# A state-space stage: tanh in place of SiLU, the norm's sums on ScalarE, another split of the state between TensorE and VectorE

## The chip, the cores and the metric

The kernel runs on one core of one Trainium2 chip. The metric is the device time of one execution in microseconds: 6,593.0 us, median of three runs (6,588.21 to 6,606.39), for the kernel before.

## The reference

The program is a decoder of two layers on an input of 128 sequences of 64 tokens with 128 features: a state-space block, an MLP, attentions, two mixtures of experts. The change touches the first block alone. What that block computes, in short:

```python
def state_space_block(x):                       # per sequence: [T=64, D=128]
    h = rmsnorm(x, input_norm_w)                # x * rsqrt(mean(x*x) + 1e-5)
    xi, z = split(h @ in_proj_W)                # 256 and 256 channels (E = 256)
    xi = silu(causal_conv4(xi) + conv_b)
    dt = clip(softplus(xi @ dt_W + dt_b), 1e-3, 0.1)
    Bt, Ct = xi @ B_W, xi @ C_W                 # N = 64 states per channel
    A = -exp(A_log)
    for t in range(T):                          # state: [E, N]
        state = exp(dt[t] * A) * state + dt[t] * xi[t] * Bt[t]
        y[t] = state @ Ct[t]
    return x + (y * silu(z)) @ out_proj_W
```

## The kernel before

The function `mamba` is the first stage of `build`; all other stages follow behind a barrier and are untouched. It goes through 16 chunks of 8 sequences. A chunk has 64 time steps `t`, of which 63 update the state (1 to 63). The state of a chunk is a [128, 1024] array in PSUM: 128 partitions are two times 64 states, 1024 columns are 4 pairs of sequences by 256 channels. Two such arrays take turns (banks UB to UB+3, by `t % 2`), a bank holds 512 columns.

In a step the engines do this:

- **TensorE**: `add_decayed(i, t)` (L1171) adds, with a product by the unit matrix, the decayed old state into columns 768 to 1023 (`PE_PART`) of the new one; `contract(i, t-1)` (L1175, products at L1183) forms the output by the C matrix; `products` (L1141) makes the step sizes for the exponential of step t+3 (decay product, L1151, bank pair DT) and the input term of step t+1 (input product, L1166). Then a side product, if the step has one. Products of 128 columns of weights go by quarters of 32 (`by_quarters`, L1134), four at a time.
- **ScalarE**: `decay` (L1380), the exponential of 1024 columns of PSUM into `dA`, a ring of four; then small copies out of the one bank PJ that side products write (`take_...`), casts, and at t = 3 the SiLU of 2048 columns (`silus`, L1407).
- **VectorE**: `decay_pe_part` (L1722, TensorE's columns: dA times old state), `add_part` (L1738, twice: its own product added to the new state of step t-1), `decay_part` (L1729, twice). Its own columns are 0 to 511 and 512 to 767 (`DVE_PARTS`). Once in 16 steps it adds the residual (`output`, L1745) and forms one small sum (`weigh_bc`, L1713), once in a chunk, at t = 24, the norm's mean square of chunk i+2 (`norm`, L1697 to L1707).
- **GpSimd**: the rest of the norm (`norm_scale`, `scale`), `step_size` (11 instructions on 1024 columns, softplus as a polynomial), the splitting of operands into three bf16 pieces (`own_rows`, `split_rest`, `split_lo`), the gate by silu(z) (`gate`).
- **SyncE**: loads, stores, and `spread_pieces`, 21 DMAs that lay the pieces out as weights.

The order is written out by hand: every engine's program is the same loop over `t`, with side work hung at fixed `tl = t % 16` of fixed quarters `j = t // 16`, and semaphores tie them. Each engine works through its queue in order. Side products for chunk i+1 and i+2 are in TensorE's queue at: turn_u at tl 1 (every quarter), project_bc at 2, turn_y at 4, project_out at 6; the step-size projections of i+1 at t = 7 to 10 and the C projection at 12, 13; the turn of i+2 at t = 40, its first conv at 42 to 45, its second at 55 to 58, the gates' product at 59, 60, 62, 63. Each group of them writes bank PJ, and the next one waits until ScalarE (or VectorE) took the one before. The waits that matter: `decay_pe_part(t)` waits for `add_decayed(t-1)`; `add_decayed(t)` for `decay_pe_part(t)`; the input product of step t+1 for all of VectorE's products of step t, as it overwrites the state that they read; the decay product of t+3 for the exponential of t+2, with one pair of banks for all.

Chunk 0 and the last three stand outside a loop, 12 chunks inside one of three iterations of four. In the last two chunks the side work for chunks that don't exist is missing.

Of the kernel before, what the change touches and what calls it, by code (L numbers as in the profile page):

```python
# [18 lines left out]
ALU = mybir.AluOpType  # L19
# [880 lines left out]
def mamba(nc, sems, ps, dram, x_in, x_out):  # L900
# [9 lines left out]
    with ExitStack() as mem:  # L910
# [42 lines left out]
        stats = st.sb("stats", [128, 4, 6])  # L953
        mv = st.sb("mv", [128, 4, 2])
# [3 lines left out]
        eps = st.sb("eps", [128, 4])  # L958
        seen = st.sb("seen", [128, 1])
# [11 lines left out]
        set_pool = st.counter("set_pool", 6)  # L971
        passed = st.counter("passed")
        sp_passed = st.counter("sp_passed")
        set_act = st.counter("set_act", 2)
# [9 lines left out]
        xz_ready = st.counter("xz_ready")  # L984
# [66 lines left out]
        with nc.Block() as block:  # L1051
# [78 lines left out]
            def _(pe):  # L1130
# [10 lines left out]
                def products(dt, ub):  # L1141
# [12 lines left out]
                    if ub:  # L1154
                        i, t = ub
                        s, tl = t // 16 % 2, t % 16
                        if t >= 2:
                            pe.wait_ge(md_ready.sem, md_ready.at(i, 2 * (t - 1)))
                        else:
                            pe.wait_ge(md_ready.sem, md_ready.at(i - 1, 2 * (T - 1 - t)))  # L1160
                        if tl == 0:
                            pieces_here(i, t // 16)
                        for pl in range(2):
                            for g in range(2):
                                k = slice(64 * g, 64 * g + 64)
                                mm = nc.tensor.matmul(ps[:, UB + 2 * (t % 2) + g, 256 * pl:256 * pl + 256],  # L1166
# [4 lines left out]
                def add_decayed(i, t):  # L1171
                    pe.wait_ge(mp_ready.sem, mp_ready.at(i, t))
                    by_quarters(state(t, PE_PART), ident, m[:, t % RING, PE_PART], False, True, False).then_inc(hp_ready.sem, 1)

# [82 lines left out]
                def first():  # L1257
# [26 lines left out]
                    products((0, 1), None)  # L1284
                    products((0, 2), (0, 0))

                def chunk(i, u, lead, lead2, trail):
                    for t in range(T):
                        j, tl = t // 16, t % 16
                        k = 4 * i + j  # L1290
                        if 1 <= t < T - 1:
                            add_decayed(i, t)
# [73 lines left out]

                def last():
# [8 lines left out]
            def _(act):  # L1376
# [5 lines left out]

                def take_turn(i):
# [8 lines left out]
                def take_conv(i, f):  # L1392
# [4 lines left out]
                                         bias=conv_b[:, f:f + 1]).then_inc(in_taken.sem, 1)  # L1397

                def take_gates(i, half):
                    act.wait_ge(in_done.sem, in_done.at(i, half + 3))  # L1400
                    nc.scalar.copy(raw[:, 1024 + 512 * half:1536 + 512 * half], ps[:, PJ, :]).then_inc(in_taken.sem, 1)
# [66 lines left out]
                def first():  # L1468
                    act.wait_ge(w_loaded.sem, w_loaded.at(0))
                    nc.scalar.copy(sel[:], sel_f[:]).then_inc(set_act.sem, 1)  # L1470
                    nc.scalar.activation(a_neg[:], a_neg[:], ACT.Exp).then_inc(set_act.sem, 1)
                    act.wait_ge(set_pool.sem, set_pool.at(0))
                    act.wait_ge(set_dve.sem, set_dve.at(0))
                    for i in range(2):
                        take_turn(i)
                        for f in range(2):
                            take_conv(i, f)
                        for half in range(2):
                            take_gates(i, half)
                        if i == 0:  # L1480
                            silus(0, 0)
# [12 lines left out]
                def chunk(i, u, lead, lead2, trail):  # L1494
                    for t in range(T):
# [5 lines left out]
                        behind = j > 0 or trail  # L1501
                        if j == 0 and tl == 0 and lead and trail:
# [6 lines left out]
                        if j == 0 and tl == 3 and lead:  # L1509
                            silus(i + 1, 1 - u)  # L1510
# [45 lines left out]
            def _(pool):  # L1556
                def norm_scale(i):
                    pool.wait_ge(normed.sem, normed.at(i))
                    nc.gpsimd.tensor_tensor(nrstd[:], msq[:], eps[:], ALU.add).then_inc(nrstd_ready.sem, 1)
# [3 lines left out]
                def scale(i):  # L1563
# [5 lines left out]
                    ins.then_inc(scaled.sem, 1)  # L1569

# [64 lines left out]
                def first():  # L1635
                    nc.gpsimd.memset(half_neg[:], -0.5).then_inc(set_pool.sem, 1)
                    nc.gpsimd.memset(eps[:], NORM_EPS).then_inc(set_pool.sem, 1)
# [6 lines left out]
                    for i in range(2):  # L1644
                        norm_scale(i)
                        scale(i)
                    for n in range(1, LP_STEPS + 1):
# [7 lines left out]
                def chunk(i, u, lead, lead2, trail):  # L1655
                    for t in range(T):
# [6 lines left out]
                        if j < 2 or lead:  # L1663
# [7 lines left out]
                            elif tl == 12:  # L1671
                                direct(ip, jp)
                        if lead and j == 0 and tl >= 11:
# [6 lines left out]
                        if lead2 and j == 1:  # L1680
                            if tl == 13:
                                norm_scale(i + 2)
                            elif tl == 14:
# [8 lines left out]
            def _(dve):  # L1692
                def norm(i):
                    dve.wait_ge(x_loaded.sem, x_loaded.at(i))
                    dve.wait_ge(nrstd_ready.sem, nrstd_ready.at(i - 1, 1))
                    for j in range(4):
                        ins = nc.vector.bn_stats(stats[:, j], x[:, j])  # L1697
                    ins.then_inc(normed.sem, 1)
                    dve.wait_ge(normed.sem, normed.at(i, 1))
                    nc.vector.tensor_copy(seen[:], stats[:, 0, 0:1])  # L1700
                    for j in range(4):
# [2311 lines left out]
```

## Time and profile before

| | |
|---|---|
| median of three runs | 6,593.0 us |
| profiled execution | 6,625.31 us |
| its span, first to last instruction | 6,623.4 us |
| VectorE busy over the span | 5,054.2 us (76%) |
| TensorE busy over the span | 5,086.3 us (77%) |
| ScalarE busy over the span | 3,374.8 us (51%) |
| GpSimd busy over the span | 3,163.8 us (48%) |
| exponentials (L1380), 1,008 of them | 1,125.2 us busy, 1,116 ns each |

In the rows DVE is VectorE, PE is TensorE (its weight loads are PEld), ACT is ScalarE, POOL is GpSimd. Instructions overlap at their ends, so the distance from start to start says what one costs in a row of them; the duration is longer.

### The profile page before, as it was taken

How to read it: one execution, taken by the hardware profiler on the slowest of the kernel's cores; microseconds unless marked ns; L12 is line 12 of the kernel's file. 1: busy time of each engine (PE TensorE's matmuls, PEld its weight loads, DVE VectorE, ACT ScalarE, POOL GpSimd, SP SyncE). 2: the span in 40 equal slices, each digit the busy share in tenths (PEclk: the TensorE clock that was granted, in tenths of full speed). 3: DMA queues.
4: the chain of work that ended last, by engine and by line, in shares of the span. 5: the costliest groups of instructions: out<-in, count | busy, mean ns of one | idle time of the engine just before them, and what ended most of it. 6: DMA issues, size and time to landing. Idle time of an engine off the chain costs nothing. (4 is left out here: it accounts for less than half of the span.)

```text
span 6623.4 us, 173241 instructions
## 1 busy us (share of the span) xinstructions
PE 5086.3 (77%) x60580; PEld 2997.0 (45%) x60580; DVE 5054.2 (76%) x10431; ACT 3374.8 (51%) x4743; POOL 3163.8 (48%) x2904
## 2 busy tenths in 40 slices
PE   4888888888888886686876965999956648777890
PEld 1333333333333334465664633666745536666440
DVE  3999999999999995697965345777769938888334
ACT  3666666666666654355751211444446617777440
POOL 5433333334443313465643564555523318889443
PEclk8999999999999998798988987999978859999995
DMA  1111111111111112221121632000011112222343
GB/s 42 41 45 47 43 46 41 49 41 40 48 41 46 42 39 82 59 58 36 44 72 55 149 106 60 18 17 18 13 29 34 28 43 73 73 73 74 121 136 102
DMA packets 620483, 368.00 MB, mean 56 GB/s; under 512 B 67337, under 2 KB 601292, under 8 KB 619852
## 3 DMA queue, kind: packets, MB, share of 16 engines
q1 hardware_dynamic: 600524, 335.54, 18.2%
q0 software_dynamic: 11648, 21.26, 1.6%
q8 instruction: 352, 5.77, 0.4%
q10 hardware_dynamic: 7680, 3.15, 0.2%
q14 instruction: 279, 2.29, 0.1%
HBM read 204.83 MB, written 66.85 MB: 41 GB/s over the span
## 5 line engine op out<-in xcount | busy, mean ns | idle before, releaser
L1380 ACT ACTIVATE mb_dA<-ps,mb_a_neg 128x1024 f32<-128x1024 f32 x1008 | 1125.2, 1116 | 905.7 <-PE ps L1151 690.0
L1729 DVE TENSOR_TENSOR mb_m<-mb_dA,ps 128x512 f32<-128x512 f32 x2016 | 1034.2, 562 | 0.0
L1738 DVE TENSOR_TENSOR ps<-mb_m,ps 128x512 f32<-128x512 f32 x1984 | 1025.8, 570 | 0.0
L1134 PE MATMUL ps<-mb_m,mb_ident 128*32 128x256 f32 x7936 | 645.7, 398 | 55.7 <-DVE mb_m L1722 55.0
L1183 PE MATMUL ps<-mb_m,mb_cz 128*32 128x256 f32 x8064 | 640.5, 390 | 16.9 <-DVE mb_m L1729 6.5
L1166 PE MATMUL ps<-mb_ur,mb_bl 64*128 64x256 bf16 x4032 | 401.8, 278 | 187.0 <-DVE mb_m L1729 175.4
L1722 DVE TENSOR_TENSOR mb_m<-mb_dA,ps 128x256 f32<-128x256 f32 x1008 | 432.5, 429 | 96.9 <-PE ps L1134 54.7
L1151 PE MATMUL ps<-mb_ur,mb_sel 64*128 64x256 bf16 x4032 | 405.1, 280 | 80.8 <-ACT mb_dA L1380 59.9
L1183 PEld LDWEIGHTS ps<-mb_m,mb_cz 128*32 128x32 f32 x8064 | 261.9, 113 | 220.7 <-issue 54.1
L1151 PEld LDWEIGHTS ps<-mb_ur,mb_sel 64*128 64x128 bf16 x4032 | 115.8, 95 | 522.7 <-issue 282.3
L1134 PEld LDWEIGHTS ps<-mb_m,mb_ident 128*32 128x32 f32 x7936 | 192.6, 110 | 320.4 <-issue 171.2
L677 POOL TENSOR_TENSOR x_p<-x_p,x_rec 128x2048 f32<-128x2048 f32 x64 | 231.8, 3622 | 211.7 <-DVE x_rec L838 211.5
L1166 PEld LDWEIGHTS ps<-mb_ur,mb_bl 64*128 64x128 bf16 x4032 | 147.1, 96 | 377.5 <-DVE mb_m L1729 364.2
L1631 POOL TENSOR_TENSOR mb_ys<-mb_ys,mb_cbu 128x256 f32<-128x256 f32 x64 | 47.0, 734 | 539.5 <-ACT mb_ys L1461 539.5
L1618 POOL TENSOR_TENSOR mb_rest<-mb_tm,mb_pc 128x768 f32<-128x768 f32 x64 | 105.8, 1653 | 366.9 <-ACT mb_pc L1439 366.9
L677 POOL TENSOR_TENSOR ea_p<-ea_p,ea_rec 128x2048 f32<-128x2048 f32 x70 | 253.6, 3622 | 37.6 <-DVE ea_rec L838 36.8
L3174 POOL TENSOR_TENSOR gq_qr<-gq_qc,gq_qs 128x1024 f32<-128x1024 f32 x64 | 151.0, 2359 | 240.1 <-DVE gq_qs L3221 222.5
L2505 POOL DMA_INDIRECT mx_tk<-moe_normed,moe_tokens x156 | 147.9, 948 | 187.6 <-POOLq L68 103.4
L487 PE MATMUL ps<-x_ident,x_p 128*128 128x128 f32 x1024 | 162.4, 310 | 61.8 <-POOL x_p L677 61.8
L599 ACT ACTIVATE x_p<-x_p 128x2048 f32<-128x2048 f32 x64 | 122.0, 1907 | 163.1 <-DVE x_p L828 163.0
L2577 DVE TENSOR_TENSOR mx_gu<-mx_gate,ps 128x512 f32<-128x512 f32 x78 | 53.5, 686 | 191.5 <-ACT mx_gate L2562 146.9
L606 ACT COPY x_pT<-ps 128x1024 f32<-128x1024 f32 x128 | 129.3, 1010 | 137.1 <-PE ps L487 136.1
(497 smaller groups left out, 13202.6 us busy)
## 6 DMA issues: line engine op xcount, KB each, us to landing
mb_ur<-mb_pc SPq DMA_DIRECT2D x768, 64.0 KB
mb_bl<-mb_pc SPq DMA_DIRECT2D x576, 64.0 KB
ef_w<-in_ef_w SPq DMA_DIRECT2D x35, 514.5 KB
mx_w<-in_mx_w SPq DMA_DIRECT2D x39, 384.0 KB
moe_made<-mx_y SPq DMA_DIRECT2D x39, 256.0 KB
ea_wqk<-in_ea_wqk SPq DMA_DIRECT2D x70, 129.0 KB
ea_wvo<-in_ea_wvo SPq DMA_DIRECT2D x70, 128.5 KB
ea_x<-hidden SPq DMA_DIRECT2D x280, 32.0 KB, 2.0
```

Source lines behind the costliest of these rows:

```text
L487: mm = nc.tensor.transpose(ps[:, 6 + c0 // 512, c0 % 512:c0 % 512 + 128], P_g[:, u, g, t, 2 * jj:2 * jj + 2, :].rearrange("p h k -> p (h k ...
L677: nc.gpsimd.tensor_tensor(v, v, rec[:].rearrange("p (c a) -> p c a", a=1).to_broadcast([128, 32, 64]), ALU.mult).then_inc(p_ready.sem, 1)
L1134: mm = nc.tensor.matmul(out[c:c + 32], weights[:, c:c + 32], moving, start=start, stop=stop, skip_group_check=not grouped)
L1151: mm = nc.tensor.matmul(ps[:, DT + g, 256 * pl:256 * pl + 256], sel[k, pl], ur[k, t // 16 % 2, t % 16], start=True, stop=True)
L1166: mm = nc.tensor.matmul(ps[:, UB + 2 * (t % 2) + g, 256 * pl:256 * pl + 256], bl[k, s, tl, 128 * pl:128 * pl + 128], ur[k, s, tl], start=g ...
L1183: mm = nc.tensor.matmul(ps[32 * pr:32 * pr + 32, YB, 0:E], cz[:, j % 2, pr, 32 * tl:32 * tl + 32], m[:, t % RING, 256 * pr:256 * pr + 256] ...
L1380: nc.scalar.activation(dA[:, t % RING].rearrange("p (g n) -> p g n", g=2), ps[:, DT:DT + 2, :], ACT.Exp, scale=a_neg[:, 0:1]).then_inc(dA_ ...
L1722: nc.vector.tensor_tensor(m[:, t % RING, PE_PART], dA[:, t % RING, PE_PART], state(t - 1, PE_PART), ALU.mult).then_inc(mp_ready.sem, 1)
L1729: nc.vector.tensor_tensor(m[:, t % RING, cols], dA[:, t % RING, cols], state(t - 1, cols), ALU.mult).then_inc(md_ready.sem, 1)
L1738: nc.vector.tensor_tensor(h, m[:, t % RING, cols], h, ALU.add).then_inc(hd_ready.sem, 1)
L2505: nc.gpsimd.indirect_dma_start(tk[:, i % DEEP, t], None, xn_rows, bass.IndirectOffsetOnAxis(ap=tokens[:, 4 * i + t:4 * i + t + 1], axis=0) ...
L3174: nc.gpsimd.tensor_tensor(qr[:, t], qc[:, t], qs[:, t], ALU.add).then_inc(q_turned.sem, 1)
```

## The change

- SiLU is made as h·tanh(h) + h with h = half the argument: ScalarE's copies into `raw` halve (`scale=0.5`, and `conv_b` is halved in the set-up), ScalarE makes tanh in four pieces of 512 columns (`tanh_half`, at t = 2, 3, 6, 7), and GpSimd multiplies and adds (`gated`, at t = 2, 4, 7, 9). `project_dt` waits piece by piece.
- The norm's sum of squares is made by ScalarE (`norm`: four Squares with a sum, at t = 26 to 29) in place of VectorE's statistics; GpSimd's `norm_scale` and `scale` come one step later.
- The parity of the state's banks is (t + u) % 2 with u the parity of the chunk, so the first state of a chunk no longer lies where the last but one of the chunk before does; the input products of a chunk's steps 0 and 1 are issued in steps 62 and 63 of the chunk before.
- TensorE's `products` (decay and input product) come behind the step's side product, not ahead of it.
- `PE_PART` is 384 columns (640 to 1023), `DVE_PARTS` are 0 to 319 and 320 to 639; the second lies over the border of two banks.

```diff
-        PE_PART = slice(768, 1024)
-        DVE_PARTS = [slice(0, 512), slice(512, 768)]
-
-        def state(t, cols):
-            g = cols.start // 512
-            return ps[:, UB + 2 * (t % 2) + g, cols.start - 512 * g:cols.stop - 512 * g]
+        PE_PART = slice(640, 1024)
+        DVE_PARTS = [slice(0, 320), slice(320, 640)]
+
+        def state(u, t, cols):
+            bank = UB + 2 * ((t + u) % 2)
+            return ps[:, bank:bank + 2, :].rearrange("p g n -> p (g n)")[:, cols]
...
                         else:
-                            pe.wait_ge(md_ready.sem, md_ready.at(i - 1, 2 * (T - 1 - t)))
+                            pe.wait_ge(md_ready.sem, md_ready.at(i - 1, 2 * (T - 2 + t)))
...
                 def project_dt(i, u, e, f):
+                    if e == 0:
+                        pe.wait_ge(xz_ready.sem, xz_ready.at(i, f + 1))
                     if f == 0:
-                        if e == 0:
-                            pe.wait_ge(xz_ready.sem, xz_ready.at(i))
-                        else:
+                        if e == 1:
                             pe.wait_ge(dtp_taken.sem, dtp_taken.at(i, 1))
...
-                        dt = (i, t + 3) if t + 3 < T else (i + 1, t + 3 - T) if lead and t + 3 > T else None
-                        ub = (i, t + 1) if t + 1 < T - 1 else (i + 1, 0) if lead and t == T - 1 else None
-                        products(dt, ub)
 
                         ahead = j < 2 or lead
                         behind = j > 0 or trail
...
                             elif tl in (11, 12, 14, 15):
                                 gates(i + 2, {11: 0, 12: 1, 14: 2, 15: 3}[tl])
 
+                        dt = (i, t + 3) if t + 3 < T else (i + 1, t + 3 - T) if lead and t + 3 > T else None
+                        if t < T - 2:
+                            products(dt, (i, t + 1) if t else None, u)
+                        else:
+                            products(dt, (i + 1, t + 2 - T) if lead else None, 1 - u)
+
...
+                def norm(i, j):
+                    act.wait_ge(x_loaded.sem, x_loaded.at(i))
+                    act.wait_ge(nrstd_ready.sem, nrstd_ready.at(i - 1, 1))
+                    act.wait_ge(xT_done.sem, xT_done.at(i - 1))
+                    nc.scalar.activation(xn[:, j], x[:, j], ACT.Square, accum_out=msq[:, j:j + 1]).then_inc(
+                        normed.sem, 1)
...
-                def silus(i, u):
-                    act.wait_ge(in_taken.sem, in_taken.at(i))
+                def tanh_half(i, u, q):
+                    act.wait_ge(in_taken.sem, in_taken.at(i, q + 1))
                     act.wait_ge(bc_done.sem, bc_done.at(4 * (i - 2) + 3))
                     act.wait_ge(yz_ready.sem, yz_ready.at(4 * (i - 2) + 3))
-                    nc.scalar.activation(xz[:, u], raw[:], ACT.Silu).then_inc(xz_ready.sem, 1)
+                    nc.scalar.activation(xz[:, u, 512 * q:512 * q + 512], raw[:, 512 * q:512 * q + 512],
+                                         ACT.Tanh).then_inc(tanh_ready.sem, 1)
...
+                def gated(i, u, q):
+                    pool.wait_ge(tanh_ready.sem, tanh_ready.at(i, q + 1))
+                    part, half = xz[:, u, 512 * q:512 * q + 512], raw[:, 512 * q:512 * q + 512]
+                    nc.gpsimd.tensor_tensor(part, part, half, ALU.mult).then_inc(xz_scaled.sem, 1)
+                    pool.wait_ge(xz_scaled.sem, xz_scaled.at(i, q + 1))
+                    nc.gpsimd.tensor_tensor(part, part, half, ALU.add).then_inc(xz_ready.sem, 1)
```

In the set-up, ahead of the first step, ScalarE's four Squares of chunk 0 wait for GpSimd's clearing of tiles, and GpSimd makes the four pieces of chunk 0 between the norm of chunk 0 and that of chunk 1.

## Rows read from the trace of the kernel before

**Rows 1.** The page: busy time by engine, and TensorE's granted clock in 40 slices.

```profile
PE 5086.3 (77%) x60580; PEld 2997.0 (45%) x60580; DVE 5054.2 (76%) x10431; ACT 3374.8 (51%) x4743; POOL 3163.8 (48%) x2904
...
PEclk8999999999999998798988987999978859999995
```

**Rows 2.** Groups by line and shape, whole span; last, the summary of line L1722.

```profile
L1722 DVE TENSOR_TENSOR mb_m<-mb_dA,ps 128x256 f32<-128x256 f32 x1008 | 432.5, 429 | 96.9 <-PE ps L1134 54.7 <-PE ps L1166 27.1 <-issue 5.9
...
L828 DVE TENSOR_TENSOR ea_p<-ps,ea_top 128x2048 f32<-128x2048 f32 x70 | 160.4, 2291 | 2.4
...
L1580 POOL TENSOR_TENSOR mb_lp<-mb_lp,mb_ex 128x1024 f32<-128x1024 f32 x64 | 151.4, 2366 | 2.8
...
L3630 ACT ACTIVATE ef_hid<-ps,ef_w 128x512 f32<-128x512 f32 x140 | 96.4, 689 | 25.8 <-PE ps L3588 24.5
...
L1425 ACT COPY mb_tm<-ps 128x512 f32<-128x512 f32 x64 | 37.5, 587 | 13.8 <-PE ps L1235 13.2
...
L1722 DVE TENSOR_TENSOR mb_m<-mb_dA,ps x1008: 410/422/517, 113.9 to 2496.3; 128x256 f32<-128x256 f32 x168
```

**Rows 3.** VectorE's timeline at the norm: start, duration (us), line, tiles, shape.

```profile
1069.64 0.42 DVE L1722 TENSOR_TENSOR mb_m<-mb_dA,ps 128x256 f32<-128x256 f32 x1
1069.97 1.02 DVE L1738 TENSOR_TENSOR ps<-mb_m,ps 128x512 f32<-128x512 f32 x2
...
1071.83 0.87 DVE L1697 BATCH_NORM_STATS2 mb_stats<-mb_x 128x6 f32<-128x128 f32 x4
...
1075.73 0.42 DVE L1722 TENSOR_TENSOR mb_m<-mb_dA,ps 128x256 f32<-128x256 f32 x1
```

**Rows 4.** Timeline of all engines over one step with a conv product.

```profile
1002.94 0.39 PE L1151 MATMUL ps<-mb_ur,mb_sel 64*128 64x256 bf16 x4
...
1003.17 0.38 PE L1166 MATMUL ps<-mb_ur,mb_bl 64*128 64x256 bf16 x4
1003.46 1.12 ACT L1380 ACTIVATE mb_dA<-ps,mb_a_neg 128x1024 f32<-128x1024 f32 x1 [0.77 <-PE ps L1151]
...
1003.48 1.07 PE L1134 MATMUL ps<-mb_xT,mb_w_conv 128*32 128x512 f32 x8
...
1004.37 0.61 PE L1134 MATMUL ps<-mb_m,mb_ident 128*32 128x256 f32 x8
...
1004.62 0.69 ACT L1395 ACTIVATE mb_raw<-ps,mb_conv_b 128x512 f32<-128x512 f32 x1
1004.80 0.61 PE L1183 MATMUL ps<-mb_m,mb_cz 128*32 128x256 f32 x8
...
1005.05 0.42 DVE L1722 TENSOR_TENSOR mb_m<-mb_dA,ps 128x256 f32<-128x256 f32 x1
1005.34 0.11 PEld L1151 LDWEIGHTS ps<-mb_ur,mb_sel 64*128 64x128 bf16 x4 [0.41 <-issue]
```

**Rows 5.** TensorE's timeline: the turn of the step-size operand and what follows.

```profile
1131.82 0.66 PE L1235 MATMUL ps<-mb_ident,mb_du 128*128 128x128 f32 x4
1132.41 0.64 PE L1134 MATMUL ps<-mb_m,mb_ident 128*32 128x256 f32 x8
```

**Rows 6.** ScalarE's timeline at the SiLU of one chunk.

```profile
1022.72 1.28 ACT L1407 ACT_TABLE_LOAD   x1
1024.01 1.91 ACT L1407 ACTIVATE mb_xz<-mb_raw 128x2048 f32<-128x2048 f32 x1
1025.94 1.28 ACT L1380 ACT_TABLE_LOAD   x1
```

**Rows 7.** VectorE's timeline over the same SiLU: the first product of three steps.

```profile
1025.37 0.42 DVE L1722 TENSOR_TENSOR mb_m<-mb_dA,ps 128x256 f32<-128x256 f32 x1
...
1029.75 0.42 DVE L1722 TENSOR_TENSOR mb_m<-mb_dA,ps 128x256 f32<-128x256 f32 x1 [2.11 <-PE ps L1134]
...
1033.74 0.41 DVE L1722 TENSOR_TENSOR mb_m<-mb_dA,ps 128x256 f32<-128x256 f32 x1
```

**Rows 8.** GpSimd's timeline in the set-up: the first step_size instruction.

```profile
56.25 2.77 POOL L1586 TENSOR_SCALAR mb_ex<-mb_ex 128x1024 f32<-128x1024 f32 x1 [18.32 <-ACT mb_ex L1417]
```

More of the change, by code:

```diff
@@ L1139, in pieces_here, with products @@
                     pe.wait_ge(pieces_loaded.of(j % 2), pieces_loaded.at(4 * i + j, j % 2))
-                def products(dt, ub):
+                def products(dt, ub, v):
                     if dt:
@@ L1283, in first @@
                     project_bc(0, 0, 1)
-                    products((0, 1), None)
-                    products((0, 2), (0, 0))
+                    products((0, 1), (0, 0), 0)
+                    products((0, 2), (0, 1), 0)
                 def chunk(i, u, lead, lead2, trail):
@@ L1471, in first @@
                     nc.scalar.activation(a_neg[:], a_neg[:], ACT.Exp).then_inc(set_act.sem, 1)
+                    nc.scalar.activation(conv_b[:], conv_b[:], ACT.Identity, scale=0.5).then_inc(set_act.sem, 1)
                     act.wait_ge(set_pool.sem, set_pool.at(0))
                     act.wait_ge(set_dve.sem, set_dve.at(0))
+                    act.wait_ge(set_act.sem, set_act.at(0))
+                    for j in range(4):
+                        norm(0, j)
                     for i in range(2):
                         take_turn(i)
+                        if i == 0:
+                            for j in range(4):
+                                norm(1, j)
                         for f in range(2):
@@ L1480, in first @@
                         if i == 0:
-                            silus(0, 0)
+                            for q in range(4):
+                                tanh_half(0, 0, q)
                             for e in range(2):
@@ L1501, in chunk @@
                         behind = j > 0 or trail
+                        if j == 1 and tl in (10, 11, 12, 13) and lead2:
+                            norm(i + 2, tl - 10)
                         if j == 0 and tl == 0 and lead and trail:
@@ L1646, in first @@
                         scale(i)
+                        if i == 0:
+                            for q in range(4):
+                                gated(0, 0, q)
                     for n in range(1, LP_STEPS + 1):
@@ L1672, in chunk @@
                                 direct(ip, jp)
+                        if lead and j == 0 and tl in (2, 4, 7, 9):
+                            gated(i + 1, 1 - u, {2: 0, 4: 1, 7: 2, 9: 3}[tl])
                         if lead and j == 0 and tl >= 11:
@@ L1692, in _ @@
             def _(dve):
[L1693 to L1701, printed above, removed]
-                        ins = nc.vector.bn_aggr(mv[:, j], stats[:, j])
-                    ins.then_inc(normed.sem, 1)
-                    dve.wait_ge(normed.sem, normed.at(i, 2))
-                    nc.vector.tensor_tensor(msq[:], mv[:, :, 0], mv[:, :, 0], ALU.mult).then_inc(normed.sem, 1)
-                    dve.wait_ge(normed.sem, normed.at(i, 3))
-                    nc.vector.tensor_tensor(msq[:], msq[:], mv[:, :, 1], ALU.add).then_inc(normed.sem, 1)
                 def weigh_bc(i, j):
@@ L1736, in add_part @@
                     cols = DVE_PARTS[g]
-                    h = state(t, cols)
+                    h = state(u, t, cols)
                     nc.vector.tensor_tensor(h, m[:, t % RING, cols], h, ALU.add).then_inc(hd_ready.sem, 1)
@@ L1772, in chunk @@
                         if t >= 1:
-                            decay_part(i, t, 0)
-                            decay_part(i, t, 1)
-                        if lead2 and j == 1 and tl == 8:
-                            norm(i + 2)
+                            decay_part(i, u, t, 0)
+                            decay_part(i, u, t, 1)
                         if tl == 11:
```

56 lines of the change are left out of this document (27 added, 29 removed).

## The prediction

> **What bounds the kernel now.** The page comes first: no engine is busy over 77% of the span [rows 1], so shares decide nothing, and the change touches one stage, the state-space scan (its first step starts at 113.9 us, its last at 2,496.3: 16 chunks of 63 steps, 1,008 in all [rows 2]). In VectorE's timeline of that stage a plain step is five instructions back to back: the TensorE part's product, 0.33 us later two sums and then two other products, 1.86 later the next instruction, 2.19 us in all and no idle [rows 3]. VectorE is the pace, and what makes a step longer is visible as a gap ahead of its first product (L1722). Over all steps these gaps sum to 96.9 us [rows 2]. A chunk takes 150 us (first to last start is 2,382 us, and the last chunks are shorter), of which 63 steps of 2.19 are 138. The other 12, by the starts of L1722 in every chunk: 3.9 at the norm on VectorE, 4.2 at the SiLU, 1.3 at the border, 2.6 in steps with side products or with small instructions of VectorE's own.
>
> **The change, part by part** (against the profiled execution, 6,625.3 us, 0.5% above the median of 6,593.0; the sum is then taken from the median).
>
> *Columns.* VectorE handles 256+768+768 = 1,792 columns a step before, 384+640+640 = 1,664 after. The starts [rows 3] give 0.33 for one instruction of 256 and 0.93 (half of 1.86) for two of together 768, so 1.05 ns a column and 0.06 an instruction: 128 columns are 0.13 us, and a step becomes 2.06. In 992 steps (a chunk's first has no sums): **-129 us**. The new slices of 320 lie over a border of PSUM banks. No row of the scan shows VectorE doing that; its instruction on 2,048 columns of PSUM passes three such borders and takes 2,291 ns, what 1.05 ns a column and a fixed part give [rows 2]. I take no penalty; the other end is 0.05 an instruction (the fixed part once more), two a step: +100.
>
> *Norm.* The 14 norms inside the scan stand between two steps of VectorE: 1,069.64 to 1,075.73 is 6.09, 3.90 over a step [rows 3]. They go: **-55**. ScalarE gets four Squares of 128 columns in four steps. No row shows one; a copy of 512 columns takes 0.59 [rows 2], an upper end, against 0.94 free beside the exponential of 1.12 in a step of 2.06. Nothing then waits for them (POOL's part is moved one step, and the turn that needs it is 20 steps on). Range 0 to +5.
> The Trainium skill (ScalarE: Activation LUTs, Rules for kernel authors) speaks against this move: multiplies belong on VectorE, which is up to three times faster. By rows a Square costs no more than 0.59 on an engine with room, and the sum has 0 for it; by the page's preference the norm would stay and the 55 us with it.
>
> *SiLU.* One activation of 2,048 columns stands with a table load before and one after between two exponentials [rows 6]; VectorE needs 8.37 for two steps (1,025.37 to 1,033.74) instead of 4.38 [rows 7], 4.2 on the mean of 15. The gap ended at TensorE's add, which waited for the exponential. These go: **-63**. In their place ScalarE makes four tanh pieces, about 0.6 each by the copy of 512. In the fullest step, 7, one stands behind a cast of 768 columns: 1.4 against 0.94 free, made good in the next two. GpSimd multiplies and adds 512 columns four times: 2.37 us for 1,024 [rows 2], so 2.4 a piece and 9.6 a chunk. GpSimd's queue is then: piece, own_rows, piece, split_rest, piece, split_lo, piece, and it is free near step 12, as the first step_size can start. The projections at steps 7 and 8 need pieces 0 and 1, ready about steps 5 and 7. Hidden; the other end is +1 a chunk, +15.
> The Trainium skill (the same page, What ACT_TABLE_LOAD costs) gives a switch 2.66 us with its drain. The load here takes 1.28 and the activation starts 0.01 behind it [rows 6], so the trace disagrees; by the page the stall would be some 2.7 larger and this term about -105.
>
> *TensorE.* Its step, in a row of start times [rows 4]: decay product to input product 0.23, to the side product 0.31, side product (conv, 512 columns) 0.89, unit product 0.43, contraction to the next decay product 0.54: 2.40, so 1.51 without a side product. The unit product has four passes on 256 columns in 0.43; 384 columns add 0.21. After: 1.72 a plain step, 2.61 with 512 columns, 2.31 with a turn (0.59 [rows 5]) and 2.18 with a short projection (about half of the conv's, 0.46). Against 2.06 TensorE loses 0.55, 0.25 and 0.12 and gains back 0.34. It may fall behind before VectorE feels it: unit product 0.60 after the step's start (the product's 0.42, 0.13 for its new columns, 0.05 for the semaphore), 0.68+0.21 = 0.88 to the next product (0.68: 1,004.37 to 1,005.05 [rows 4]), so 2.06-1.48 = 0.58.
> The new order puts the side product ahead of the decay product, and thus of ScalarE's exponential. Where one side product needs the bank that ScalarE clears of the one before (steps 1 to 2 of every 16, 8 to 9, and 10 to 11 in the last 16), the way is: decay product to exponential 0.52, exponential 1.12, take 0.59 to 0.69, 2.3 to 2.4 with the semaphores; TensorE is back there after 0.23+0.31+0.64+0.54 = 1.72. It waits 0.6 to 0.7.
> Going through a chunk with these: 0.38 at each step 2 (four times); the dt and c group (steps 7 to 13) 0.09+0.55+1.24+0.55+0.21+0.55; the first conv group 0.52+0.55+0.55; the second with the gates 0.09+3x0.55+0.78+0.09. That is 9.5 with the steps at 2; VectorE's own small instructions in the same steps hide 1.3, so 8.2; before, the same groups cost 1.4. So 6.9 in each of 14 chunks, 4 in the 15th, about nothing in the last: **+101**. Ends: +54 if the waits for ScalarE don't come (3.7 a chunk), +160 if nothing of TensorE's lag is hidden (11.3).
>
> *Border.* With the parity kept over it, the next chunk's first input product no longer waits for the last product. L1722's idle behind L1166 is 27.1 us over the run [rows 2], about 0.6 at each of 12 plain borders and more at the first steps; it goes, but the second step still waits for unit product, contraction and exponential in a row. **-7**, between -20 and +5.
>
> *Set-up.* GpSimd stood idle 18.32 us until step_size [rows 8]. Now four pieces (9.6) and the second norm (about 3.5) stand before it, which began 4 us ahead of that point, and ScalarE's first Squares wait for GpSimd's clearing. **+6**, between 0 and +10.
>
> Sum: -129-55-63+101-7+6 = -147. From 6,593: **6,446 us**, 2.2% faster.
>
> **Rivals.**
> *TensorE keeps up*: the waits for ScalarE fall into slack; +54 instead of +101: 6,399. For it: most single side products now leave no mark at 2.19. Against: conv steps are at 2.40 now [rows 4], and they get longer.
> *Nothing is hidden*: +160 instead of +101: 6,505. For it: the lag allowed is only 0.58. Against: two of four conv steps are absorbed now.
> *The table loads stay*: tanh not in the exponential's table. Each piece would bring two loads, 1.12+2.57+0.6 in a step of 2.06, some 9.3 a chunk where 4.2 is now: +77 instead of -63 is +140, 6,586, no change. Against: the Relu of a later stage runs behind exponentials with idle time that TensorE alone ends, no load [rows 2].
> The Trainium skill (ScalarE: Activation LUTs, Table sets) lists tanh and relu in the set of exp, which gives this rival its small chance; no run here shows tanh.
> *ScalarE and TensorE in a ring, slower than before*: every side product, not six of 35 in a chunk, waits for ScalarE, because the exponential now starts behind the side product and each take behind the exponential. 29 more waits of 0.7 in 15 chunks are +300: 6,750. It decides from 147/(29x15) = 0.34 us for each. Against: most side products have a step without one behind them, and TensorE's way to the second next is 3.4, over the 2.4 needed.
>
> **How the numbers follow.** Forecast 0.56, TensorE keeps up 0.19, nothing hidden 0.14, table loads stay 0.04, ring 0.05, else 0.02 (a penalty at the bank border is in the last and in the third). The range takes the first three with their bounds, 6,385 to 6,510; the small ends of norm, SiLU and border lie in it. A measurement of this kernel tells 0.3% (20 us) from no change: faster 0.90, within 0.05, slower 0.05.
>
> **What would show it.** L1722's starts 2.06 apart in plain steps; products of 320 columns near 0.49 each, or longer if the bank border costs; no load of a table between 122 and 2,230 us; no gap at steps 6 and 24; periods of 2.6 in conv steps; TensorE idle behind ScalarE's copy at steps 2 and 9. TensorE's granted clock, nine tenths with some eights in the stage's slices [rows 1], should be no lower, as long idle stretches at steps 6 and 24 are gone. The prediction is wrong if plain steps are not at 2.06, or if side steps cost far from 7 us a chunk more.

## The result: 1.4% faster, with more of the gain eaten than forecast

The changed kernel takes 6,504.2 us (median), the kernel before 6,591.9 measured beside it: ratio 0.9857, 95% interval 0.9838 to 0.9876, so 82 to 107 us less. The forecast was 6,446, in a range of 6,385 to 6,510. Two executions of one later run (ScalarE's copies first) took more than twice the usual time, 14,057 and 14,334 us, and are left out. The profiled execution has a span of 6,481.9 us. Its page of the profile:

```profile
PE 5194.2 (80%) x60580; PEld 2995.8 (46%) x60580; DVE 4876.1 (75%) x10255; ACT 3334.8 (51%) x4888; POOL 3324.5 (51%) x3031
...
PEclk8999999999999998898979977999978859999995
```

VectorE has lost 178 us of work against [rows 1], TensorE has gained 108, GpSimd 161; the granted clock in the stage's slices is as before. The groups by line that answer to [rows 2] (the first two parts of VectorE's work and its sums):

```profile
L1739 DVE TENSOR_TENSOR mb_m<-mb_dA,ps 128x384 f32<-128x384 f32 x1008 | 552.8, 548 | 191.4 <-PE ps L1132 140.3 <-ACT mb_dA L1381 40.7 <-issue 9.0
L1746 DVE TENSOR_TENSOR mb_m<-mb_dA,ps 128x320 f32<-128x320 f32 x2016 | 883.7, 479 | 0.0
L1755 DVE TENSOR_TENSOR ps<-mb_m,ps 128x320 f32<-128x320 f32 x1984 | 879.1, 488 | 0.0
...
L1739 DVE TENSOR_TENSOR mb_m<-mb_dA,ps x1008: 537/547/556, 117.6 to 2400.3; 128x384 f32<-128x384 f32 x168
```

Where VectorE waited 96.9 us ahead of its first product [rows 2], it now waits 191.4, nearly all for TensorE's unit product (L1132) and for the exponential (L1381). The scan starts 3.7 us later (117.6 against 113.9) and its last step starts 96.0 earlier (2,400.3 against 2,496.3). The medians are 88 apart, so the scan has the whole of the change. The spans of the two profiled executions are 141.5 apart, and should not be compared: 45.5 of that lies behind the scan, in stages that the change does not touch. These stages take 4,082 us in this one execution, 4,127 in the kernel before and 4,120 to 4,132 in all runs below; why they were shorter here stays open.

The starts of VectorE's first product in each of the 63 steps, in medians over the 12 chunks of the loop, add up to this (us per chunk; the length of step t is the distance to the start of the next one; the forecast's column is put together here from the terms of its steps, 2.06 for a plain one, with VectorE's own small instructions as measured):

| steps | before | after | forecast |
|---|---|---|---|
| border: 63, 1, 2, 3 | 9.37 | 10.52 | 8.7 |
| 4 to 8 (the SiLU's) | 15.68 | 10.49 | 10.5 |
| 9 to 15 (dt and c projections) | 15.87 | 17.50 | 17.5 |
| second and third of the other quarters: 18, 19, 34, 35, 50, 51 | 13.13 | 15.13 | 13.5 |
| 43 to 47 (first conv) | 11.46 | 11.99 | 11.9 |
| 57 to 62 (second conv, gates) | 13.62 | 14.89 | 14.9 |
| the other 30 (with the norm's step) | 70.57 | 62.42 | 62.5 |
| all | 149.70 | 142.95 | 139.5 |

Two lines, the border and the quarters, hold the whole miss of 3.4 us a chunk: 1.8 and 1.6. One quarter's start in full, in the timeline of all engines (start, duration, idle before and what ended it):

```profile
1021.59 0.54 DVE L1739 TENSOR_TENSOR mb_m<-mb_dA,ps 128x384 f32<-128x384 f32 x1
...
1021.86 1.12 ACT L1381 ACTIVATE mb_dA<-ps,mb_a_neg 128x1024 f32<-128x1024 f32 x1 [0.71 <-PE ps L1149]
...
1022.19 0.85 PE L1132 MATMUL ps<-mb_m,mb_ident 128*32 128x384 f32 x8
...
1022.88 0.36 ACT L1471 COPY mb_ys<-ps 128x256 f32<-128x256 f32 x1
...
1023.34 0.64 PE L1181 MATMUL ps<-mb_m,mb_cz 128*32 128x256 f32 x8 [0.30 <-issue]
1023.64 0.55 DVE L1739 TENSOR_TENSOR mb_m<-mb_dA,ps 128x384 f32<-128x384 f32 x1
1023.91 0.66 PE L1233 MATMUL ps<-mb_ident,mb_du 128*128 128x128 f32 x4
...
1025.96 0.55 DVE L1739 TENSOR_TENSOR mb_m<-mb_dA,ps 128x384 f32<-128x384 f32 x1 [0.18 <-PE ps L1132]
1026.02 0.58 ACT L1435 COPY mb_tm<-ps 128x512 f32<-128x512 f32 x1
...
1026.65 0.64 PE L1132 MATMUL ps<-mb_w_bc,mb_xz 128*32 128x128 f32 x16 [0.33 <-ACT mb_tm L1435]
...
1028.69 0.56 DVE L1739 TENSOR_TENSOR mb_m<-mb_dA,ps 128x384 f32<-128x384 f32 x1 [0.59 <-PE ps L1132]
```

TensorE waits twice for ScalarE. The unit product starts at 1,022.19; the contraction behind it could start 0.66 later, at 1,022.85, but it opens a new sum in the one bank for outputs and waits until ScalarE has copied the old one out. That copy (L1471) stands behind the exponential and ends at 1,023.24; the contraction starts at 1,023.34. (The view puts the last 0.30 of this gap down to "issue"; the kernel has the wait, and the run with ScalarE's copies first, below, takes it away.) Then the projection at 1,026.65 waits for the copy (L1435) of the turn ahead of it. The second wait was in the forecast, the first was not, and both fall in a stretch where TensorE has no lag to spare: 2.31 and 2.73 us for two steps of 2.06.

The border, same view:

```profile
1126.03 0.55 DVE L1739 TENSOR_TENSOR mb_m<-mb_dA,ps 128x384 f32<-128x384 f32 x1
...
1126.38 1.12 ACT L1381 ACTIVATE mb_dA<-ps,mb_a_neg 128x1024 f32<-128x1024 f32 x1 [0.57 <-PE ps L1149]
...
1127.55 0.39 PE L1149 MATMUL ps<-mb_ur,mb_sel 64*128 64x256 bf16 x4 [0.41 <-ACT mb_dA L1381]
1127.87 0.85 PE L1132 MATMUL ps<-mb_m,mb_ident 128*32 128x384 f32 x8
...
1128.79 0.55 DVE L1739 TENSOR_TENSOR mb_m<-mb_dA,ps 128x384 f32<-128x384 f32 x1 [1.41 <-PE ps L1132]
1129.08 0.59 ACT L1409 ACTIVATE mb_raw<-ps 128x512 f32<-128x512 f32 x1
...
1129.71 0.66 PE L1233 MATMUL ps<-mb_ident,mb_du 128*128 128x128 f32 x4 [0.99 <-ACT mb_raw L1409]
```

Step 1 starts with no gap, as the new parity should have it. But the decay product of step 3 stands ahead of the unit product of step 1 in TensorE's queue, and it waits for the exponential of step 2: the gap is now ahead of step 2, 1.41 us. Behind it the turn at step 1, now ahead of the products, waits 0.99 for the copy of the gates.

### The profile page after: what moved, and what is told of

Same layout as the page of the kernel before. It is cut to its first block and busy times, and to the rows that moved or that the text cites. A ratio compares the mean times of both kernels' runs of the same rounds, so it can differ in the third digit from the quotient of the medians.

```text
span 6481.9 us, 173452 instructions
## 1 busy us (share of the span) xinstructions
PE 5194.2 (80%) x60580; PEld 2995.8 (46%) x60580; DVE 4876.1 (75%) x10255; ACT 3334.8 (51%) x4888; POOL 3324.5 (51%) x3031
## 3 DMA queue, kind: packets, MB, share of 16 engines
q10 hardware_dynamic: 7680, 3.15, 0.2%
## 5 line engine op out<-in xcount | busy, mean ns | idle before, releaser
L1381 ACT ACTIVATE mb_dA<-ps,mb_a_neg 128x1024 f32<-128x1024 f32 x1008 | 1123.9, 1115 | 858.7 <-PE ps L1149 800.5
L1746 DVE TENSOR_TENSOR mb_m<-mb_dA,ps 128x320 f32<-128x320 f32 x2016 | 883.7, 479 | 0.0
L1755 DVE TENSOR_TENSOR ps<-mb_m,ps 128x320 f32<-128x320 f32 x1984 | 879.1, 488 | 0.0
L1132 PE MATMUL ps<-mb_m,mb_ident 128*32 128x384 f32 x7936 | 848.9, 500 | 23.1 <-DVE mb_m L1739 5.6
L1739 DVE TENSOR_TENSOR mb_m<-mb_dA,ps 128x384 f32<-128x384 f32 x1008 | 552.8, 548 | 191.4 <-PE ps L1132 140.3
L1181 PE MATMUL ps<-mb_m,mb_cz 128*32 128x256 f32 x8064 | 623.0, 381 | 23.0 <-issue 11.9
L1132 PEld LDWEIGHTS ps<-mb_m,mb_ident 128*32 128x32 f32 x7936 | 156.3, 108 | 254.5 <-DVE mb_m L1739 159.0
L1164 PEld LDWEIGHTS ps<-mb_ur,mb_bl 64*128 64x128 bf16 x4032 | 172.5, 94 | 98.5 <-DVE mb_m L1746 79.3
L606 ACT COPY ea_pT<-ps 128x1024 f32<-128x1024 f32 x140 | 141.6, 1012 | 94.2 <-PE ps L487 91.8
```

The source lines that it names most:

```text
L606: nc.scalar.copy(pT[:, t], ps[:, 6:8, :].rearrange("p a n -> p (a n)")).then_inc(pT_ready.sem, 1)
L1132: mm = nc.tensor.matmul(out[c:c + 32], weights[:, c:c + 32], moving, start=start, stop=stop, skip_group_check=not grouped)
L1164: mm = nc.tensor.matmul(ps[:, UB + 2 * ((t + v) % 2) + g, 256 * pl:256 * pl + 256], bl[k, s, tl, 128 * pl:128 * pl + 128], ur[k, s, tl], s ...
L1181: mm = nc.tensor.matmul(ps[32 * pr:32 * pr + 32, YB, 0:E], cz[:, j % 2, pr, 32 * tl:32 * tl + 32], m[:, t % RING, 256 * pr:256 * pr + 256] ...
L1381: nc.scalar.activation(dA[:, t % RING].rearrange("p (g n) -> p g n", g=2), ps[:, DT:DT + 2, :], ACT.Exp, scale=a_neg[:, 0:1]).then_inc(dA_ ...
L1739: nc.vector.tensor_tensor(m[:, t % RING, PE_PART], dA[:, t % RING, PE_PART], state(u, t - 1, PE_PART), ALU.mult).then_inc(mp_ready.sem, 1)
```

## The experiments

A chunk's length is always the sum over 63 steps as in the table. Ratios are to the kernel before, measured beside it on the same chip; the changed kernel stands at 0.9857 and 142.95.

**Products first.** The new order of TensorE's queue undone, nothing else:

```diff
+                        dt = ...
+                        if t < T - 2:
+                            products(dt, (i, t + 1) if t else None, u)
+                        ...
                         ahead = j < 2 or lead
...  (side products)
-                        if t < T - 2:
-                            products(dt, (i, t + 1) if t else None, u)
```

> The changed kernel with one part undone: decay and input product stand ahead of the step's side product again. Theory (the new order makes TensorE wait for ScalarE, since the exponential starts behind the side product: 0.33 to 0.6 at steps 2 of every 16, 0.65 at steps 9 and 59, 1.0 at step 1): those waits go, a chunk falls from 143.0 to about 138.5 us and the time from 6,504 to about 6,440. Rival (the new order hides side products in TensorE's idle time ahead of the input product): a chunk rises to about 145 and the time to about 6,535, the conv groups lose most.

Ratio 0.9788 (0.9772 to 0.9804), a chunk 139.80. The quarters' starts fall from 15.13 to 13.52, the border from 10.52 to 9.45, steps 9 to 15 by 0.6, 57 to 62 by 0.6; in the steps where a group begins the new order was worth 0.1 to 0.2 (steps 8, 43 and 44, 56). The groups of TensorE's side products that wait for ScalarE, after and here:

```profile
L1132 PE MATMUL ps<-mb_w_bc,mb_xz 128*32 128x128 f32 x1024 | 42.5, 285 | 23.5 <-ACT mb_tm L1435 23.5
...
L1132 PE MATMUL ps<-mb_w_in,mb_xT_tok 128*32 128x256 f32 x512 | 39.1, 382 | 9.0 <-ACT mb_raw L1403 7.5 <-ACT mb_raw L1409 1.4
```

```profile
L1132 PE MATMUL ps<-mb_w_bc,mb_xz 128*32 128x128 f32 x1024 | 42.1, 283 | 5.0 <-ACT mb_tm L1434 5.0
...
L1132 PE MATMUL ps<-mb_w_in,mb_xT_tok 128*32 128x256 f32 x512 | 40.1, 390 | 3.1 <-ACT mb_raw L1402 1.6 <-ACT mb_raw L1408 1.4
```

The idle time ahead of the projection falls from 23.5 to 5.0 us. The theory holds in kind, with 3.2 us a chunk in place of 4.5 and some 45 us in place of 64; the rival is out.

**ScalarE's copies first.** The output's copy and, at step 0, the gates' copy ahead of that step's exponential, TensorE's order as in the change:

```diff
+                        if j == 0 and tl == 0 and lead and trail:
+                            take_gates(i + 1, 1)
+                        if tl == 0 and behind:
+                            take_y(...)
                         if t + 3 < T:
                             decay(i, t + 3)
```

> The changed kernel with ScalarE's copies at the start of a quarter (the output's, and the second gates' copy at step 0) ahead of that step's exponential, nothing else. Theory (the contraction that opens a quarter waits 0.5 for the output's copy behind the exponential, and the turn at step 1 waits 1.0 for the gates' copy): steps 18, 34, 50 go from 2.31 to 2.06 and the next ones from 2.73 to about 2.45, step 2 falls by 0.7 or more, a chunk from 143.0 to about 140, the time by 40 us. Rival (the copies delay the exponential and with it the next decay product by as much): a chunk within 0.5 of 143.

A chunk 140.45. Steps 18, 34, 50 are at 2.06, the next ones at 2.49 (were 2.31 and 2.73), step 2 falls from 2.98 to 2.06. Its time rests on two executions, 6,495.8 and 6,497.6 against 6,625.8, which is 0.9805 with no interval; the steps are read from the trace. So the wait that the forecast lacked is shown by taking it away: 0.5 at each of three quarters and 1.0 at the border.

**Both.** 

> The changed kernel with products ahead of side products and with ScalarE's copies at a quarter's start ahead of the exponential. Theory (two waits of TensorE for ScalarE, one behind the other): a chunk from 139.8 with the first alone to about 138.3, a ratio to before of 0.975 to 0.977. Rival (with the old order the lag that the copy makes is worked off anyway): a chunk at 139.5 to 140, 0.979.

Ratio 0.9764 (0.9748 to 0.9781), a chunk 138.77: another 1.03 on top of products first, where the theory had 1.5 and the rival 0.3 at most. One by one the two moves gave 3.15 and 2.50, together they give 4.18, not 5.65: they take away some of the same waits.

**256 columns.** The change with `PE_PART = slice(768, 1024)` and `DVE_PARTS` 0 to 383, 384 to 767:

> The changed kernel with one part undone: TensorE's unit product takes 256 columns again, VectorE's parts are 0 to 383 and 384 to 767. Plain steps go back to 2.19 us by both. Theory (TensorE's lag in side steps has eaten the columns' gain): conv steps at 2.40, groups at steps 2 and 3 nearly plain, a chunk at 142 to 143.5, the time within 15 us of 6,504. Rival (the columns are what gains, 0.13 in most steps): a chunk at 147 or more, the time 6,560 to 6,630.

Ratio 0.9839 (0.9823 to 0.9856), a chunk 141.53, shorter than with 384. Plain steps are at 2.19 and quarters' starts as well; the wait of TensorE stays within its lag. The conv steps 44 to 46, which follow a product of the conv, are at 2.19 too, where the theory had 2.40. The waits at the border (steps 2 and 3 at 2.98 and 2.73) and at step 10 (2.74) stay. The part of the change that looked like its core was worth nothing in it, or a little less: the chunk is 1.4 longer with it, and the intervals of the two ratios overlap.

**The columns alone,** on the kernel before, in its order and with its SiLU and norm:

```diff
-        PE_PART = slice(768, 1024)
-        DVE_PARTS = [slice(0, 512), slice(512, 768)]
+        PE_PART = slice(640, 1024)
+        DVE_PARTS = [slice(0, 320), slice(320, 640)]
```

> The kernel before with one part of the change alone: 384 columns for TensorE's unit product, 320 and 320 for VectorE. Theory (the columns gain 0.13 in VectorE's steps and lose 0.21 in each step that TensorE sets, and half-clock steps behind the SiLU and the norm go from about 2.3 to 3.2): plain steps 2.06, a chunk of 149 stays within 2 us, the time within 25 us of before. Rival (in the old order and with no other part the columns pay by themselves): a chunk at 145 or less, 60 us faster than before.

Ratio 0.9997 (0.9987 to 1.0006), a chunk 150.15 against 149.70: nothing, as the theory had it. Plain steps are at 2.06, and what they gain is lost again: 2.4 us in steps 9 to 15, 43 to 47 and 57 to 62, 0.4 at the quarters' starts, and 1.3 in steps 24 to 26, where the norm stands on VectorE.

**Columns in the good order.** Both moves from above, and 256, 320, 384, 448 columns for TensorE, VectorE's two parts half of the rest each.

> The kernel with products ahead of side products and ScalarE's copies first, with 256 columns for TensorE, 384 and 384 for VectorE. Theory (the columns pay once TensorE no longer waits for ScalarE: what 384 lost to 256 in the changed kernel was that wait, not the product's 0.21 us): plain steps 2.19, a chunk at 140.3 to 141.3 where 384 gave 138.8, a ratio to before of 0.980 to 0.983. Rival (256 is as good as 384 in any order): a chunk at 139.5 or less, 0.978 or less.

> The same with both moves, and 320 columns for TensorE, 352 and 352 for VectorE. Theory (each 64 columns give 0.066 in some 48 steps and take 0.107 in some 14, and less is hidden): plain steps 2.12 to 2.13, steps with conv 2.50 to 2.51, a chunk about 1 us longer than with 384, 15 us slower. Rival (TensorE's steps weigh more than counted): as fast as 384 or faster.

> The kernel with products ahead of side products and ScalarE's copies first, now with 448 columns for TensorE, 288 and 288 for VectorE. Theory (TensorE's way to the next product has grown so that the lag allowed falls to some 0.35 us): plain steps 2.00, steps with conv 2.72, a chunk within 0.7 of 138.8, the time within 10 us of the same kernel with 384. Rival (the slope from 320 to 384, 0.9 a chunk, goes on): a chunk at 138.0 or less, 13 us faster.

| TensorE's columns | plain step | conv step | chunk | ratio (interval) |
|---|---|---|---|---|
| 256 | 2.19 | 2.40 | 141.18 | 0.9837 (0.9817 to 0.9856) |
| 320 | 2.12 | 2.51 | 139.67 | 0.9795 (0.9779 to 0.9812) |
| 384 | 2.06 | 2.62 | 138.77 | 0.9764 (0.9748 to 0.9781) |
| 448 | 2.00 | 2.72 | 141.12 | 0.9817 (0.9800 to 0.9833) |

With each 64 columns a plain step gets 0.065 shorter and a conv step 0.107 longer, at all four sizes. 384 is worth 2.4 us a chunk over 256 here, and cost 1.4 in the changed kernel: the size was right, the queue was not ready for it. Seen the other way, the two moves are worth 4.18 a chunk with 384 columns and 0.35 with 256 (141.53 to 141.18). At 448 I had the sum near zero; it is +2.35. The quarters' starts take 0.9 more than with 384, steps 43 to 47 and 9 to 15 0.6 each, 57 to 62 0.5, and even single side products show (steps 5, 21, 37 at 2.10, step 8 at 2.54). That fits the lag of only 0.35 us that the expectation estimates; no run isolates it.

**SiLU back.** One activation with its table loads in place of the four pieces:

> The changed kernel with one part undone: one SiLU of 2,048 columns with its two table loads, no tanh pieces and no work of GpSimd for them. Theory (the pieces cost nothing, the stall was 4.2 in 15 chunks): steps 6 and 7 take 8.5 to 9, the time rises by 60 to about 6,565, the scan starts 3 to 4 us earlier. Rival (the pieces cost part of that where ScalarE or GpSimd is full): it rises by 40 or less.

Ratio 0.9969 (0.9958 to 0.9979): 1.1% or some 74 us back, more than the 60 of the theory. Steps 6 to 8 take 6.05, 3.37 and 2.61; the chunk is 148.67, 5.7 longer. On the mean of 15 chunks the stall costs 5.4 us over plain steps and the output's own 0.2, against 4.8 in the columns alone and 4.0 in the kernel before (the 4.2 of the forecast has the output in it). So some 0.8 of the extra goes with the columns; the rest comes with other parts of the change, and no run says which. The granted clock is lower behind this stall as well, 0.57 from 1,029 to 1,033 us (0.56 from 1,029 to 1,032 in the kernel before), after 5 us in which TensorE was busy for 2.11:

```profile
1029.00:1033.00 4.00, 3.50 (x34) 1.58 (x38) 0.99 (x3) 2.54 (x4) 0.89 (x1) 0.57 0.00 0
```

The scan starts 3.2 us earlier. No table load stands in the scan of the changed kernel, and the pieces cost nothing: with them steps 4 to 8 are plain but for the output's 0.19, and steps 9 to 15 take 17.50 against 17.54 here.

**Norm back.** VectorE's statistics at step 24 in place of ScalarE's Squares:

> The changed kernel with one part undone: the norm's sums on VectorE at step 24. Theory (3.9 us in 14 chunks in which TensorE has no lag to work off): step 24 takes 6.0, the time rises by 54 to about 6,558. Rival (part of the 2.2 us of one small product of the norm is contention with GpSimd and would be shorter at the new place in GpSimd's queue): it rises by 30 or less.

Ratio 0.9970 (0.9957 to 0.9982), again some 75 us, where the theory had 54. A chunk is 148.76, 5.8 longer. VectorE's timeline shows 6.52 us for step 24, of which 3.1 are two products of four columns:

```profile
1075.06 0.88 DVE L1727 TENSOR_TENSOR mb_msq<-mb_mv 128x4 f32<-128x4 f32 x1
1075.97 2.26 DVE L1729 TENSOR_TENSOR mb_msq<-mb_msq,mb_mv 128x4 f32<-128x4 f32 x1
1078.15 0.54 DVE L1744 TENSOR_TENSOR mb_m<-mb_dA,ps 128x384 f32<-128x384 f32 x1
```

In the kernel before, step 24 takes 6.09, and only one of the two is long (2.24 and 0.16): the rival's contention with GpSimd is there, but it costs more at the new place, not less (see the last section). The windows at the pause and behind it (TensorE, its loads, VectorE, ScalarE, GpSimd busy; granted clock; DMA) show TensorE at 0.50, the lower level of 1.2 GHz, after 6 us in which it was busy for 2.15:

```profile
1072.00:1078.00 6.00, 2.15 (x28) 0.64 (x24) 5.90 (x16) 2.79 (x3) 6.00 (x3) 0.98 0.08 22
1078.00:1080.30 2.30, 1.55 (x12) 0.59 (x16) 2.28 (x6) 0.00 (x0) 2.08 (x2) 0.50 0.03 7
1080.30:1083.50 3.20, 3.20 (x28) 1.03 (x24) 2.14 (x5) 1.61 (x3) 3.12 (x2) 0.50 0.00 0
```

A plain step at half clock is set by TensorE and takes 3.23 us (step 26) with 384 columns. The kernel before took 2.26 there, at a granted clock of 0.50 too. So the long pause costs a second time, and more with the new split: of the 5.8, 4.5 are step 24 and 1.2 step 26. The columns alone had the same (3.26).

**Parity back.** Banks by `t % 2`, the next chunk's first input product in step 63:

> The changed kernel with one part undone: the state's banks by t alone, the next chunk's first input product issued in step 63 and its second in step 0. Theory (at the border the way of unit product, contraction and exponential sets the pace, and an input product that is ready earlier only waits): the four steps 63, 1, 2, 3 sum to 10.5 as now, give or take 0.3, the time within 8 us of the changed kernel. Rival (the border part saves what the forecast gave it or more): the sum rises by 0.5 or more, the time by 8 to 20 us.

Ratio 0.9860 (0.9843 to 0.9877), a chunk 142.96 against 142.95, the border's four steps 10.52 both times. Without the new order it is worth nothing either: the four steps take 9.45 in the columns alone, which has the old parity, and 9.45 with products first, which has the new one (the two differ in the norm and the SiLU as well). In the changed kernel the gaps only lie elsewhere; with the parity back they are 0.59 ahead of step 1, for the input product, and 0.95 ahead of step 2:

```profile
1127.81 0.55 DVE L1737 TENSOR_TENSOR mb_m<-mb_dA,ps 128x384 f32<-128x384 f32 x1 [0.59 <-PE ps L1164]
...
1130.11 0.55 DVE L1737 TENSOR_TENSOR mb_m<-mb_dA,ps 128x384 f32<-128x384 f32 x1 [0.95 <-PE ps L1132]
```

**The best of it.** Copies first; products first but for the step that opens a group of side products and those with the output projection; in the set-up the second norm ahead of the tanh pieces on GpSimd:

```diff
+                        side_first = tl == 6 or (j in (0, 3) and tl == 7) or (j == 2 and tl == 10)
+                        if not side_first:
+                            step_products()
...  (side products)
+                        if side_first:
+                            step_products()
```

> Products ahead of side products except in the first step of a group of side products and where VectorE waits for the output projection (steps 6 of every 16, 7, 42, 55), ScalarE's copies first, and in the set-up the second norm ahead of the four tanh pieces' products. Theory (side first is worth its place only where the next side product does not wait for ScalarE): 0.8 us less a chunk than with products always first, a chunk at 138.0, the scan's start 2 to 4 us earlier, a ratio to before of 0.974. Rival (the lag saved at the first step is paid at the second): a chunk at 138.7 or more, 0.976.

Ratio 0.9747 (0.9729 to 0.9766): 1.1% under the changed kernel, 2.5% under the one before. A chunk is 138.11, and the scan starts at 115.3 us instead of 118.1 in the run with both moves. Most of that is the two moves; of the mix (0.66 a chunk, 10 us) only the profile speaks, as its interval overlaps that of both moves.

## Why the prediction was right, and where it was off

- **Columns**: right. Plain steps are at 2.06, which over 992 steps is the -129 of the forecast; products of 320 columns take 479 ns, and the one over the border of two banks costs nothing more.
- **Norm and SiLU**: right against the kernel before (steps 24 and 6, 7 are plain but for the output's own 0.19), -55 and -63. ScalarE's Squares take 0.30 us and the read of their sum 0.19, below the 0.59 of the forecast, a tanh piece 0.62. Taken back they cost 75 and 74. For the norm the runs show why: a second product of VectorE meets GpSimd, and the step at half clock behind it is longer with 384 columns (3.23 for 2.26). For the SiLU they show it only in part. The forecast had no term for either, as it had no stall left to cause one. The rule of the Trainium skill (ScalarE: Activation LUTs, Rules for kernel authors) that stood against moving the squares, multiplies on VectorE, has its factor of three for bf16 with one source; the squares are fp32, and on VectorE they cost these 75 us.
- **TensorE in groups**: the steps were right where they were counted. A conv step takes 2.62, the steps that wait for a copy 3.26 and 2.83 (forecast 2.61, 3.30, 2.84), and the groups came out within 0.1 us a chunk. The sum of the term was not: the excesses listed add up to 8.9, not to 9.5, so that by its own working the term is +91 and the forecast 6,436. (In the rival of the table loads 4 times 2.23 is 8.9, not 9.3.) What was measured is more than either: side steps cost 10.9 over plain ones against 2.7 before, so 8.2 a chunk more where the forecast had 6.9. Most of the difference lies in the next step.
- **Quarters' starts**: the step that failed. The forecast took 0.38 for each step 2 and overlooked what the contraction waits for when it opens a new sum: ScalarE's copy of the output, 0.5 us more with the lag then gone. The table has 1.6 a chunk too much in three quarters. With the copies first the two steps exceed plain ones by 0.43, close to the 0.38. In the kernel before this wait was there too, inside the lag that TensorE was allowed; with 384 columns in the old order step 18 is at 2.31.
- **Border**: the second failure. The four steps were forecast at 8.7, less than before; measured is 10.52 for 9.37, so +17 us over 15 chunks. The parity alone, forecast at -7, is worth zero: the gap ahead of step 1 goes (0.59 with the old parity), and the one ahead of step 2 grows from 0.95 to 1.41. There unit product, contraction and exponential follow each other, a way that the forecast named and gave too little. The columns cost 0.08 of the 1.15 (9.45 in the columns alone), TensorE's new order 1.07 (9.45 with products first): the turn at step 1, moved ahead, meets the gates' copy, which the forecast had not seen, and the copies first take 0.99 of it away as well.
- **Set-up**: +3.7 for +6.
- The forecast's sum was -147; its last step came 96 earlier. 1.6 and 1.8 us in each of 15 chunks are these 51.
- **Rivals**: "nothing is hidden" has 6,505 and the measurement 6,504, but that is chance. Its mechanism is not there: steps 5, 21, 37 and 53, with a single side product, are at 2.06, and the excess over the forecast came from two waits that neither counted. "TensorE keeps up" is out: the waits for ScalarE are there. Of the ring of ScalarE and TensorE, priced at 0.34 us for every side product to make the change slower, a part is there: waits of 0.3 to 1.0 us came at more places than counted, but most side products had none. The table loads did not come: no such instruction stands in the scan. The Trainium skill (ScalarE: Activation LUTs, Table sets) lists tanh in the set of exp, and the trace agrees.

The sum of one queue's steps was worked out correctly, and the waits between queues were looked up only where a side product follows a side product. Every wait in the queue counts once the lag allowed shrinks from about 1.04 us (2.19-0.47-0.68, an estimate by the forecast's own working for 256 columns) to 0.58.

## What to carry to other kernels

When work moves to an engine that is second to the bound, list each wait in its queue and the lag that hides it now: a split by columns is worth its arithmetic only after those waits are out of the way (here 384 columns lost 1.4 us a chunk in one order and gained 2.4 in another). Put the producer of another engine's long instruction ahead of work that only this engine needs, and a copy that frees a single bank ahead of a long instruction on its own engine. A stall can cost more than its length where the clock falls behind it: with the norm back 1.2 of 5.8 us a chunk were one step at half clock behind the pause.

## What the runs showed of the hardware that I had not expected

- VectorE's product of two tiles in SBUF, four columns wide, takes 0.16 us when no product of GpSimd runs beside it, and otherwise lasts until GpSimd's product ends: 2.23 to 2.28 us in all 14 norms of the scan of the kernel before, 0.88 and then 2.26 in the run with the norm back. There it ends at 1,075.97 + 2.26 = 1,078.23, and GpSimd's product, started at 1,075.87, at 1,078.21:

```profile
1075.87 2.34 POOL L1597 TENSOR_TENSOR mb_lp<-mb_lp,mb_ex 128x1024 f32<-128x1024 f32 x1
```

  The same holds in the kernel before, where the second product comes after GpSimd's has ended, and is short:

```profile
1073.08 2.34 POOL L1580 TENSOR_TENSOR mb_lp<-mb_lp,mb_ex 128x1024 f32<-128x1024 f32 x1
1073.20 2.24 DVE L1705 TENSOR_TENSOR mb_msq<-mb_mv 128x4 f32<-128x4 f32 x1
1075.47 0.16 DVE L1707 TENSOR_TENSOR mb_msq<-mb_msq,mb_mv 128x4 f32<-128x4 f32 x1
```

  Beside a memset of GpSimd, in the set-up (20.04 to 23.55 us), the product keeps its 0.16. VectorE's products with one operand in PSUM keep 0.55 and 0.48 us beside GpSimd's products. The Trainium skill (GPSIMD Engine Reference, 1. Specifications) says that GpSimd shares its SBUF interface with VectorE and contends with VectorE's instructions that read two inputs there; the rows agree, and show it as a wait for the whole instruction.
- GpSimd's instructions of 512 columns, in the changed kernel's groups by line, take 1,282 ns (median), 8% more than half of one of 1,024 [rows 2]:

```profile
L1596 POOL TENSOR_TENSOR mb_xz<-mb_xz,mb_raw x64: 1265/1282/1297, 46.4 to 2153.3; 128x512 f32<-128x512 f32 x64
```

- A VectorE instruction whose slice lies over two PSUM banks costs what its columns cost: of L1746's 2,016 products half lie in one bank and half over two, and both halves have a mean of 479 ns.
